# A drain behind the last matmul of every group gives TensorE's signals, in a two-layer graph network

## The chip, the cores and the metric

One core of one Trainium2 chip runs the whole program in one launch. The metric is the device time of one execution in microseconds, as the median of several runs. Engines are named as in the profile: PE (TensorE; PEld are its weight loads), DVE (VectorE), ACT (ScalarE), POOL (GpSimd), SP (SyncE).

## The reference, cut to what matters

The input is `x` (8 x 2048 x 256, float32) and an adjacency matrix `adj` (8 x 2048 x 2048, int32, here of zeros and ones, about 1.6% ones, with ones on the diagonal). Two layers follow each other:

```python
# layer 0: of each row, the first 25 neighbours; their features' maximum
vals, idx = jax.lax.top_k(where(adj != 0, -arange(N), -inf), 25)
agg = max over the 25 of x[idx]            # with 0 among them when the degree is <= 25
x = layernorm(x + relu(concat([x, agg]) @ W0 + b0))
# layer 1: four heads of 64, attention over the neighbours
h = einsum('bnd,hde->bhne', x, W1)
weight = leaky_relu(e_src[i] + e_dst[j]) where adj == 1, else -1e9
dst = softmax(weight) @ h + bias
out = per-head layernorm(relu(dst) + h) * gamma + beta
x = layernorm(x + out)
```

## The kernel before, in words

The 16384 rows are 128 tiles of 128 rows (`TILES`); four tiles (`QT`) are a quad, and 16 tiles are one batch entry. Each engine runs its own loop over quads (`run_quads`), and in it one `step(quad, u)` for each tile `u` of the quad. There is no scheduler: the order of the work on each engine is the order in which `step` writes it, and engines meet by semaphores alone. A wait compares a semaphore with a count worked out from the quad's number.

The stages stand at different tiles in one step:

- **Masks and search**, ahead. ACT turns an adjacency tile into float16 (line 518), PE transposes it in 16 pieces in two halves (line 1148, `transpose_mask`), ACT copies each half into `stage` and into the ring `maskT` (lines 543 and 547), PE packs 16 columns to a word with 16 short matmuls (line 1162, `pack_words`), and DVE finds the first 26 neighbours in a chain of 35 operations, each of which waits for the one before it (`search_words` from line 729, `top32` at lines 716 and 718, up to `idx` at line 769). Line 731 tells PE that the words are read.
- **Gather**. POOL issues 25 indirect DMAs to a tile (line 499), five to a chunk. DVE takes the maximum chunk by chunk (line 837) and frees each chunk for POOL as it goes (`s_rfree`); then it reduces (lines 846 and 847). PE transposes `x` and `agg` (line 1188, `transpose_xa`) and ACT copies the result (line 629).
- **Layer 0's product and norm**. PE multiplies (lines 1201 and 1202, `product0`), DVE adds the residual and normalizes (lines 779 to 811), PE transposes again (line 1211), ACT copies (line 641), PE multiplies by layer 1's weights (lines 1217 and 1219, `product1`), ACT takes the exponentials (lines 654 to 664, `project`).
- **Attention**, one batch entry behind. A tile's step has eight units. For a unit ACT scales two blocks (line 566), DVE masks them (line 820), and PE multiplies two heads (line 1233, `attend`). Four buffers `uv` are passed round, so ACT's unit n waits until PE is done with unit n - 4.
- **A quad's end**. At `u == 0` ACT moves the sums out of PSUM (line 587), PE transposes them (line 1172, `back`), DVE divides (lines 861 and 864, `divide`), and only then may PE start the next quad's sums (line 868 tells it); the finishing work stands between DVE's other operations.

```python
back (u == 0); product0; units 0-3; product1; units 4, 5;
transpose_mask; unit 6; pack_words; transpose_xa; unit 7
```

Of the kernel before, what the change touches and what calls it, by code (L numbers as in the profile page):

```python
# [29 lines left out]
P = 128  # L30
B, N, C = 8, 2048, 256
HEADS, HO = 4, 64
HW = HO + 1
S = 25
JT = N // P
# [10 lines left out]
WPT = P // WORD  # L46
# [106 lines left out]
def layers_program(nc, x, adj, w0, b0, w1, a_src, a_dst, bias1, gamma, beta,  # L153
# [12 lines left out]
    with ctx:  # L166
        def sb(name, shape, dt):
            return ctx.enter_context(nc.sbuf_tensor(name, shape, dt))

        def ps(name, shape, dt):  # L170
            return ctx.enter_context(nc.psum_tensor(name, shape, dt))

        def sem(name):
            return ctx.enter_context(nc.semaphore(name))

        id16 = sb("id16", [P, P], F16)
        id32 = sb("id32", [P, P], F32)
        pack = sb("pack", [P, WPT], BF16)
# [5 lines left out]
        b0_sb = sb("b0_sb", [1, C], F32)  # L185
        ones_row = sb("ones_row", [1, P], F32)
        wcat = sb("wcat", [P, 2, C + 2 * HEADS], F32)
# [8 lines left out]
        mask_sb = sb("mask_sb", [P, N], F16)  # L196
        stage = sb("stage", [P, JT, P], BF16)
# [22 lines left out]
        xh = [sb(f"xh{p}", [P, 2, C], F32) for p in range(2)]  # L220
        x1T = sb("x1T", [P, 2, P], F32)
        hs = sb("hs", [P, 2 * JT, HEADS, HW], F32)
# [6 lines left out]
        uv = [sb(f"uv{k}", [P, 2, IB], F32) for k in range(UVB)]  # L229
        sT = sb("sT", [HW, HEADS, IB], F32)  # L230
# [34 lines left out]
        acc = [ps(f"acc{i}", [P, 512], F32) for i in range(QT)]  # L265
        pT = [ps(f"pT{i}", [P, HALF * P], F16) for i in range(2)]
        pA = ps("pA", [P, 512], F32)
        pB = ps("pB", [P, 512], F32)
        p_lin, p_key = pB[:, 0:C], pB[:, 384:384 + WORDS]
        p_h = pB[:, 0:C + 2 * HEADS]  # L270
        p_ed = pB[:, C + HEADS:C + 2 * HEADS]
        p_x1T, p_es = pA[:, 0:2 * P], pA[0:HEADS, 2 * P:3 * P]
# [8 lines left out]
        s_T = sem("s_T")  # L281
        s_stage = sem("s_stage")
        s_ring = sem("s_ring")
        s_key = sem("s_key")
# [7 lines left out]
        s_xaT = sem("s_xaT")  # L292
        s_xaE = sem("s_xaE")
        s_lin = sem("s_lin")
# [7 lines left out]
        s_x1T = sem("s_x1T")  # L302
        s_x1E = sem("s_x1E")
        s_h = sem("s_h")
# [5 lines left out]
        s_pe = sem("s_pe")  # L310
        s_blk = sem("s_blk")
        s_sT = sem("s_sT")
        s_back = sem("s_back")
# [820 lines left out]
        def _(pe):  # L1134
# [3 lines left out]
            def transpose_mask(quad, u, g_of):  # L1138

                for v in quad.reach(lambda q: QT * q + u + g_of + 1):  # L1140
                    pe.wait_ge(s_mask, v)
                for hf in range(2):

                    for v in quad.reach(lambda q: 2 * (QT * q + u + g_of - 1) + hf + 1):
                        pe.wait_ge(s_ring, v)
                    for j in range(HALF):
                        jt = hf * HALF + j
                        last = nc.tensor.transpose(pT[hf][:, j * P:(j + 1) * P], mask_sb[:, jt * P:(jt + 1) * P], id16[:])
                    last.then_inc(s_T, 1)

            def pack_words(quad, u, g_of):

                for v in quad.reach(lambda q: 2 * (QT * q + u + g_of + 1)):
                    pe.wait_ge(s_stage, v)
                for v in quad.reach(lambda q: QT * q + u + g_of):
                    pe.wait_ge(s_keyread, v)

                for v in quad.reach(lambda q: QT * q + u + g_of - FRONT):
                    pe.wait_ge(s_proj, v)  # L1160
                for jt in range(JT):
                    last = nc.tensor.matmul(p_key[:, jt * WPT:(jt + 1) * WPT], stage[:, jt, :], pack[:], start=True, stop=True)
                last.then_inc(s_key, 1)

            def back(quad):

                for v in quad.reach(lambda q: q - BQ):
                    pe.wait_ge(s_sT, v)
                for i in range(QT):  # L1170
                    for h in range(HEADS):
                        last = nc.tensor.transpose(acc[i][:, h * HW:(h + 1) * HW], sT[:, h, i * P:(i + 1) * P], id32[0:HW, 0:HW])
                last.then_inc(s_back, 1)

            def transpose_xa(quad, u):

                p = u % 2

                for v in quad.reach(lambda q: QT * q + u + 1):
                    pe.wait_ge(s_agg, v)  # L1180
                for v in quad.reach(lambda q: 16 * (2 * q + u // 2 + 1)):
                    pe.wait_ge(s_x[p], v)

                for v in quad.reach(lambda q: QT * q + u):
                    pe.wait_ge(s_proj, v)
                for c in range(4):
                    src = (xt[p] if c < 2 else agg)[:, c % 2 * P:(c % 2 + 1) * P]
                    last = nc.tensor.transpose(pA[:, c * P:(c + 1) * P], src, id32[:])  # L1188
                last.then_inc(s_xaT, 1)

            def product0(quad, u):

                if quad.on(u, -AHEAD):
                    for v in quad.reach(lambda q: QT * q + u + AHEAD + 1):
                        pe.wait_ge(s_keyread, v)

                for v in quad.reach(lambda q: QT * q + u):
                    pe.wait_ge(s_xaE, v)
                for c in range(4):  # L1200
                    nc.tensor.matmul(p_lin, xaT[:, c, :], w0_sb[:, c, :], start=(c == 0), stop=False)  # L1201
                nc.tensor.matmul(p_lin, ones_row[:], b0_sb[:], start=False, stop=True).then_inc(s_lin, 1)

            def product1(quad, u):

                p = (u - 1) % 2

                for v in quad.reach(lambda q: QT * q + u):
                    pe.wait_ge(s_x1, v)
                for c in range(2):  # L1210
                    last = nc.tensor.transpose(p_x1T[:, c * P:(c + 1) * P], xh[p][:, 0, c * P:(c + 1) * P], id32[:])  # L1211
                last.then_inc(s_x1T, 1)

                for v in quad.reach(lambda q: QT * q + u):
                    pe.wait_ge(s_x1E, v)
                for c in range(2):
                    nc.tensor.matmul(p_h, x1T[:, c, :], wcat[:, c, :], start=(c == 0), stop=(c == 1))  # L1217
                for c in range(2):
                    last = nc.tensor.matmul(p_es, wcat[:, c, C:C + HEADS], x1T[:, c, :], start=(c == 0), stop=(c == 1))
                last.then_inc(s_h, 1)  # L1220

            def attend(quad, u, a, b):

                if not quad.on(u, QT * BQ):
                    return
                for n in range(a, b):
                    jt, hh, k = QT * u + n // 2, n % 2, n % UVB

                    for v in quad.reach(lambda q: UNITS * (q - BQ) + US * u + n + 1):
                        pe.wait_ge(s_u, v)  # L1230
                    for i in range(2):
                        h = 2 * hh + i
                        last = nc.tensor.matmul(acc[h][0:HW, :], hs[:, (1 - quad.par) * JT + jt, h, :], uv[k][:, i, :],  # L1233
                                                start=(jt == 0), stop=(jt == JT - 1))
                    last.then_inc(s_pe, 1)

            def step(quad, u):
                if u == 0 and quad.on(u, FIN):
# [23 lines left out]
            for g in range(FRONT):  # L1262
                transpose_mask(Quad(pe, 0, 0, 0), 0, g)
                pack_words(Quad(pe, 0, 0, 0), 0, g)
# [7 lines left out]
            with pe.If(pe.value_load(redo[0:1, 0:1], min_val=0, max_val=1) > 0):  # L1272
                with pe.Fori(0, TILES) as g:

                    pe.wait_ge(s_g1load, 16 * g + 16)
                    for c in range(2):
                        last = nc.tensor.transpose(pA[:, c * P:(c + 1) * P], xr[:, 0, c * P:(c + 1) * P], id32[:])
# [5 lines left out]
                    for c in range(2):  # L1283
                        last = nc.tensor.matmul(pA[0:TH, 2 * P:3 * P], wst[:, (2 * c + 1) * TH:(2 * c + 2) * TH], x1T[:, c, :],
                                                start=(c == 0), stop=(c == 1))
                    last.then_inc(s_g1P, 1)
                with pe.Fori(0, TILES) as g:
                    for h in range(HEADS):

                        pe.wait_ge(s_g2p, HEADS * g + h + 1)  # L1290
                        for j in range(JT):
                            last = nc.tensor.transpose(acc[j // QT][:, j % QT * P:(j % QT + 1) * P], z[:, j * P:(j + 1) * P], id32[:])
# [3 lines left out]
                        for j in range(JT):  # L1296
                            last = nc.tensor.matmul(pA[:, 0:HO], pTs[:, j * P:(j + 1) * P], hb[:, j * C + h * HO:j * C + (h + 1) * HO],
                                                    start=(j == 0), stop=(j == JT - 1))
# [52 lines left out]
```

## Time and profile before

| | |
|---|---|
| median of 3 runs | 5537.12 us (5534.57 to 5538.47) |
| the profiled execution | 5509.0 us, its span 5507.2 us |
| PE busy | 3399.5 us, 62% |
| DVE busy | 4129.9 us, 75% |
| ACT busy | 3106.5 us, 56% |
| POOL busy | 3739.9 us, 68% |
| mean granted clock of PE | 0.776 |
| HBM | 692.79 MB moved, mean 126 GB/s |

How to read it: busy time leaves out the sequencer's work, so POOL's 68% doesn't hold the part of each indirect DMA that stands in the profile as idle time before it ("issue").
### The profile page before, as it was taken

The numbers are of one execution on the slowest core, as the hardware profiler recorded it, in microseconds if no ns is written. First come the engines' busy times: TensorE is split into PE (matmuls) and PEld (weight loads), VectorE is DVE, ScalarE is ACT, GpSimd is POOL, SyncE is SP. The second block draws the span as 40 slices with busy tenths as digits, with TensorE's granted clock in tenths as the row PEclk, the third lists the DMA queues.
The fourth block names the chain that finished last, engine by engine and source line by source line (L and its number), as shares of the span: only waits on it lengthen the run. The fifth ranks groups of instructions, "written<-read, shape, count | busy, mean of one in ns | idle before, by whom it ended". The sixth has DMA issues, their size and how long they took to land.

```text
span 5507.2 us, 58308 instructions
## 1 busy us (share of the span) xinstructions
PE 3399.5 (62%) x11778; PEld 1421.4 (26%) x11778; DVE 4129.9 (75%) x11484; ACT 3106.5 (56%) x5570; POOL 3739.9 (68%) x3204
## 2 busy tenths in 40 slices
PE   1233266676666765666666666675576665756786
PEld 1112122222222322222222222222222222322222
DVE  4455468787787876978877877786788787967777
ACT  3233356565565655656655665664566565755565
POOL 4666677777787776877776777776677776877400
PEclk9555577787877877878877877777787787877898
DMA  3333344444444444434444444443444444444210
GB/s 122 116 121 114 121 141 132 140 123 137 133 146 127 143 133 124 146 123 148 135 134 127 144 131 129 135 142 112 132 135 150 123 135 127 146 128 129 81 38 27
DMA packets 282031, 692.79 MB, mean 126 GB/s; under 512 B 62849, under 2 KB 130178, under 8 KB 265346
## 3 DMA queue, kind: packets, MB, share of 16 engines
q0 software_dynamic: 153600, 419.64, 26.2%
q1 hardware_dynamic: 128130, 270.41, 15.1%
q14 instruction: 267, 2.19, 0.1%
q8 instruction: 34, 0.56, 0.0%
HBM read 639.21 MB, written 50.59 MB: 125 GB/s over the span
## 4 chain that ended last, share of the span: by engine, by line
DVE 27%; issue 19%; POOL 16%; PE 15%; another core or an unknown queue 12%; ACT 9%; DMA 1%; ACTq 0%; DVEq 0%; POOLq 0%; SPq 0%
POOL rows L499 16%; PE acc L1233 8%; DVE uv L820 8%; DVE rmax L837 4%; ACT uv L566 4%; DVE top L716 2%; PE pB L1201 2%; DVE agg L846 2%; DVE key_b L718 2%; PE pB L1217 1%; ACT stage L526 1%; ACT maskT L547 1%; DMA rows<-in_x_dram,idx 1%; DVE key_a L718 1%
## 5 line engine op out<-in xcount | busy, mean ns | idle before, releaser
L499 POOL DMA_INDIRECT rows<-in_x_dram,idx x3200 | 3739.7, 1169 | 1437.6 <-issue 1039.0
L1233 PE MATMUL acc<-uv,hs 128*65 128x512 f32 x4096 | 2253.1, 700 | 562.3 <-DVE uv L820 326.7
L820 DVE SCALAR_TENSOR_TENSOR uv<-uv,maskT 128x1024 f32<-128x1024 f32 x1024 | 1241.2, 1222 | 390.3 <-ACT uv L566 245.2
L566 ACT ACTIVATE uv<-rb,qj 128x512 f32 (+1 forms) x2048 | 1327.4, 711 | 240.0 <-PE acc L1233 143.6
L1233 PEld LDWEIGHTS acc<-uv,hs 128*65 128x65 f32 x4096 | 596.1, 158 | 1836.4 <-issue 1410.3
L837 DVE TENSOR_TENSOR rmax<-rmax,rows 128x1280 f32<-128x1280 f32 x384 | 569.2, 1482 | 118.2 <-DMA rows<-in_x_dram,idx 106.0
L1201 PE MATMUL pB<-w_sb,xaT 128*128 128x256 f32 x1024 | 369.0, 523 | 294.0 <-DVE pad L731 153.7
L629 ACT ACTIVATE xaT<-pA 128x512 f32<-128x512 f32 x128 | 76.4, 597 | 728.8 <-remote 392.6
L543 ACT ACTIVATE stage<-pT 128x1024 bf16<-128x1024 f16 x256 | 258.9, 1011 | 255.8 <-remote 142.8
L1201 PEld LDWEIGHTS pB<-w_sb,xaT 128*128 128x128 f32 x1024 | 264.9, 270 | 454.1 <-DVE pad L731 211.2
L596 ACT ACTIVATE sd<-mv,eps 128x1 f32<-128x1 f32 x128 | 37.7, 295 | 515.7 <-DVE tick L792 433.6
L846 DVE TENSOR_REDUCE agg<-rmax 128x256 f32<-128x1280 f32 x128 | 299.2, 2337 | 7.4 <-remote 1.6
L1188 PE MATMUL pA<-id,xt 128*128 128x128 f32 x256 | 75.9, 392 | 360.8 <-DVE agg L847 211.1
L641 ACT ACTIVATE x1T<-pA 128x256 f32<-128x256 f32 x128 | 49.1, 383 | 420.6 <-PE pA L1211 242.2
L1211 PE MATMUL pA<-id,xh 128*128 128x128 f32 x256 | 64.4, 340 | 349.0 <-DVE xh L811 336.6
L1217 PE MATMUL pB<-wcat,x1T 128*128 128x264 f32 x512 | 196.7, 520 | 118.8 <-ACT x1T L641 70.3
L547 ACT ACTIVATE maskT<-pT 128x1024 f16 (+1 forms) x256 | 258.8, 1011 | 0.0
L779 DVE SCALAR_TENSOR_TENSOR r<-pB,xt 128x256 f32<-128x256 f32 x128 | 53.3, 416 | 272.8 <-remote 189.0
L526 ACT ACTIVATE stage<-adj_sb,minus 128x2048 bf16<-128x2048 int32 x128 | 254.3, 1986 | 1.2 <-remote 1.2
L518 ACT ACTIVATE mask_sb<-adj_sb 128x2048 f16<-128x2048 int32 x128 | 243.0, 1898 | 3.7 <-DMA adj_sb<-in_adj_dram 3.2
L716 DVE MAX8 top<-key_a 128x8 f32<-128x104 f32 (+1 forms) x768 | 209.9, 273 | 40.9 <-remote 8.6
L716 DVE MAX8 top<-key_b 128x8 f32<-128x104 f32 (+1 forms) x768 | 207.4, 270 | 41.6 <-remote 24.7
(113 smaller groups left out, 3904.5 us busy)
## 6 DMA issues: line engine op xcount, KB each, us to landing
adj_sb<-in_adj_dram SPq DMA_DIRECT2D x128, 1024.0 KB
rows<-in_x_dram,idx POOLq DMA_INDIRECT x3200
xh_dram<-xh SPq DMA_DIRECT2D x128, 256.0 KB
rb<-r_dram SPq DMA_DIRECT2D x32, 1024.0 KB
xr<-xh_dram SPq DMA_DIRECT2D x64, 512.0 KB
xt<-in_x_dram SPq DMA_DIRECT2D x128, 128.0 KB
out_dram<-xr SPq DMA_DIRECT2D x32, 512.0 KB
r_dram<-er SPq DMA_DIRECT2D x128, 2.0 KB
```

The costliest lines, as they stand in the source:

```text
L499: nc.gpsimd.indirect_dma_start(rows[:, c, r * C:(r + 1) * C], None, x_rows, bass.IndirectOffsetOnAxis(ap=idx[u][:, k:k + 1], axis=0)).then ...
L526: nc.scalar.activation(stage[:].rearrange("p j i -> p (j i)"), adj_sb[:], ACT.Square, scale=2.0, bias=minus1[:], accum_out=adj_sq[:, bass. ...
L543: nc.scalar.activation(stage[:, hf * HALF:(hf + 1) * HALF, :], src, ACT.Square).then_inc(s_stage, 1)
L547: nc.scalar.activation(maskT[:, bass.ds(qg % RING * JT + hf * HALF, HALF), ug * P:(ug + 1) * P], src, ACT.Square).then_inc(s_ring, 1)
L566: last = nc.scalar.activation(uv[k][:, i, :], rb[:, bass.ds(qa % 2, 1), h, :].rearrange("p a i -> p (a i)"), ACT.Copy, scale=q_j(h))
L716: ch.then(nc.vector.max(top[:, k:k + 8], a))
L820: nc.vector.scalar_tensor_tensor(uv[k][:], uv[k][:], 1.0, m, ALU.max, ALU.mult).then_inc(s_u, 1)
L837: nc.vector.tensor_tensor(rmax[:], before, rows[:, c, :], ALU.max).then_inc(s_rfree, 2 if c == 1 else 1)
L846: ch.then(nc.vector.tensor_reduce(agg[:], rmax[:].rearrange("p (r f) -> p f r", f=C), axis=AX.X, op=ALU.max))
L1201: nc.tensor.matmul(p_lin, xaT[:, c, :], w0_sb[:, c, :], start=(c == 0), stop=False)
L1217: nc.tensor.matmul(p_h, x1T[:, c, :], wcat[:, c, :], start=(c == 0), stop=(c == 1))
L1233: last = nc.tensor.matmul(acc[h][0:HW, :], hs[:, (1 - quad.par) * JT + jt, h, :], uv[k][:, i, :], start=(jt == 0), stop=(jt == JT - 1))
```

## The change

Each group's increment is taken off its last matmul and put on a drain that follows it on PE's queue. The drain is an instruction of its own in PE's queue: it is to pass when the engine has finished what was given to it before, and then it gives the increment. The order of matmuls, all waits and all counts stay as they are; no other engine's program changes. One place stands for all, with the two that read otherwise:

```diff
                     for j in range(HALF):
                         jt = hf * HALF + j
-                        last = nc.tensor.transpose(pT[hf][:, j * P:(j + 1) * P], mask_sb[:, jt * P:(jt + 1) * P], id16[:])
-                    last.then_inc(s_T, 1)
+                        nc.tensor.transpose(pT[hf][:, j * P:(j + 1) * P], mask_sb[:, jt * P:(jt + 1) * P], id16[:])
+                    pe.drain().then_inc(s_T, 1)
...
-                nc.tensor.matmul(p_lin, ones_row[:], b0_sb[:], start=False, stop=True).then_inc(s_lin, 1)
+                nc.tensor.matmul(p_lin, ones_row[:], b0_sb[:], start=False, stop=True)
+                pe.drain().then_inc(s_lin, 1)
...
                     for i in range(2):
                         h = 2 * hh + i
-                        last = nc.tensor.matmul(acc[h][0:HW, :], hs[:, (1 - quad.par) * JT + jt, h, :], uv[k][:, i, :],
+                        nc.tensor.matmul(acc[h][0:HW, :], hs[:, (1 - quad.par) * JT + jt, h, :], uv[k][:, i, :],
                                                 start=(jt == 0), stop=(jt == JT - 1))
-                    last.then_inc(s_pe, 1)
+                    pe.drain().then_inc(s_pe, 1)
```

`s_key`, `s_back`, `s_xaT`, `s_x1T` and `s_h` are changed in the same way. Over the program that is 8 x 128 + 7 x 128 + 32 = 1952 drains.

## Rows read from the trace of the kernel before

**Rows 1.** The page: busy time of each engine, granted clock, chain that ended last.

```profile
span 5507.2 us, 58308 instructions
...
PE 3399.5 (62%) x11778; PEld 1421.4 (26%) x11778; DVE 4129.9 (75%) x11484; ACT 3106.5 (56%) x5570; POOL 3739.9 (68%) x3204
...
PEclk9555577787877877878877877777787787877898
...
DVE 27%; issue 19%; POOL 16%; PE 15%; another core or an unknown queue 12%; ACT 9%; DMA 1%; ACTq 0%; DVEq 0%; POOLq 0%; SPq 0%
```

**Rows 2.** The page's groups: busy, mean ns | idle before, releaser.

```profile
L499 POOL DMA_INDIRECT rows<-in_x_dram,idx x3200 | 3739.7, 1169 | 1437.6 <-issue 1039.0
...
L1233 PE MATMUL acc<-uv,hs 128*65 128x512 f32 x4096 | 2253.1, 700 | 562.3 <-DVE uv L820 326.7
```

**Rows 3.** The waits, whole span: who waited for whom, us, times, longest.

```profile
POOL rows L499 <- DVE rmax L837: 355.3, 40, 16.8
...
ACT xaT L629 <- remote: 392.6, 32, 29.0
...
DVE r L779 <- remote: 189.0, 31, 21.5
...
DVE key_b L729 <- remote: 165.9, 19, 26.2
...
ACT stage L543 <- remote: 142.8, 35, 17.1
...
DVE rden L861 <- remote: 89.6, 11, 13.4
...
POOL rows L499 <- DVE idx L769: 43.4, 1, 43.4
```

**Rows 4.** Timeline, 1963 to 1989 us: start, us, engine, line [idle before <-releaser].

```profile
1965.72 2.00 PE L1172 MATMUL acc<-id,sT 65*128 65x65 f32 x16 [9.36 <-issue]
...
1967.51 3.73 PE L1201 MATMUL pB<-w_sb,xaT 128*128 128x256 f32 x8
...
1971.17 0.88 PE L1202 MATMUL pB<-b_sb,ones_row 1*128 1x256 f32 x2
...
1981.66 0.39 DVE L861 RECIPROCAL rden<-acc 128x4 f32<-128x4 f32 x4 [13.45 <-remote]
...
1988.39 0.94 POOL L499 DMA_INDIRECT rows<-in_x_dram,idx  x1 [10.49 <-DVE rmax L837]
```

**Rows 5.** Timeline, 263 to 273 us.

```profile
262.36 0.59 PE L1162 MATMUL pB<-pack,stage 128*128 128x8 bf16 x16 [29.07 <-ACT stage L543]
...
263.27 0.63 PE L1188 MATMUL pA<-id,agg 128*128 128x128 f32 x2
...
267.60 0.95 POOL L499 DMA_INDIRECT rows<-in_x_dram,idx  x1 [0.30 <-issue]
...
272.58 0.29 DVE L729 SCALAR_TENSOR_TENSOR key_b<-pB,wordkey 128x128 f32<-128x128 f32 x1 [15.58 <-remote]
...
272.64 0.60 ACT L629 ACTIVATE xaT<-pA 128x512 f32<-128x512 f32 x1 [9.42 <-remote]
```

**Rows 6.** Timeline of a step without such a wait, 3000 to 3028 us.

```profile
3000.09 0.38 PE L1211 MATMUL pA<-id,xh 128*128 128x128 f32 x2
...
3000.51 0.38 ACT L641 ACTIVATE x1T<-pA 128x256 f32<-128x256 f32 x1 [2.23 <-PE pA L1211]
...
3000.94 1.16 PE L1217 MATMUL pB<-wcat,x1T 128*128 128x264 f32 x4 [0.47 <-ACT x1T L641]
...
3006.30 1.93 PE L1233 MATMUL acc<-uv,hs 128*65 128x512 f32 x4 [1.81 <-DVE uv L820]
...
3013.00 3.43 PE L1233 MATMUL acc<-uv,hs 128*65 128x512 f32 x4 [3.87 <-DVE uv L820]
...
3025.75 7.08 PE L1233 MATMUL acc<-uv,hs 128*65 128x512 f32 x16
```

**Rows 7.** Windows: two steps without such a wait, and the one of rows 4.

```profile
core 0: us, PE busy (x) PEld busy (x) DVE busy (x) ACT busy (x) POOL busy (x), PEclk, DMA share, GB/s
...
3166.00:3201.20 35.20, 25.46 (x88) 10.33 (x88) 32.44 (x79) 23.43 (x43) 28.12 (x23) 0.84 0.41 127
...
3201.20:3236.10 34.90, 25.29 (x88) 10.20 (x88) 30.60 (x83) 25.01 (x44) 27.91 (x23) 0.79 0.41 128
...
1964.00:2008.00 44.00, 25.89 (x96) 12.02 (x96) 23.71 (x69) 20.83 (x39) 26.51 (x25) 0.72 0.33 103
```

**Rows 8.** Window of the tail after the last gather, line 1233 alone.

```profile
5190.00:5507.00 317.00, 236.52 (x516) 71.35 (x516) 0.90 0.12 38
```

**Rows 9.** Timeline of PE within the tail.

```profile
5301.14 13.95 PE L1233 MATMUL acc<-uv,hs 128*65 128x512 f32 x32 [0.73 <-DVE uv L820]
5317.03 17.71 PE L1233 MATMUL acc<-uv,hs 128*65 128x512 f32 x40 [1.93 <-DVE uv L820]
```

More of the change, by code:

```diff
@@ L1161, in pack_words @@
                 for jt in range(JT):
-                    last = nc.tensor.matmul(p_key[:, jt * WPT:(jt + 1) * WPT], stage[:, jt, :], pack[:], start=True, stop=True)
-                last.then_inc(s_key, 1)
+                    nc.tensor.matmul(p_key[:, jt * WPT:(jt + 1) * WPT], stage[:, jt, :], pack[:], start=True, stop=True)
+                pe.drain().then_inc(s_key, 1)
             def back(quad):
@@ L1171, in back @@
                     for h in range(HEADS):
-                        last = nc.tensor.transpose(acc[i][:, h * HW:(h + 1) * HW], sT[:, h, i * P:(i + 1) * P], id32[0:HW, 0:HW])
-                last.then_inc(s_back, 1)
+                        nc.tensor.transpose(acc[i][:, h * HW:(h + 1) * HW], sT[:, h, i * P:(i + 1) * P], id32[0:HW, 0:HW])
+                pe.drain().then_inc(s_back, 1)
             def transpose_xa(quad, u):
@@ L1187, in transpose_xa @@
                     src = (xt[p] if c < 2 else agg)[:, c % 2 * P:(c % 2 + 1) * P]
-                    last = nc.tensor.transpose(pA[:, c * P:(c + 1) * P], src, id32[:])
-                last.then_inc(s_xaT, 1)
+                    nc.tensor.transpose(pA[:, c * P:(c + 1) * P], src, id32[:])
+                pe.drain().then_inc(s_xaT, 1)
             def product0(quad, u):
@@ L1210, in product1 @@
                 for c in range(2):
-                    last = nc.tensor.transpose(p_x1T[:, c * P:(c + 1) * P], xh[p][:, 0, c * P:(c + 1) * P], id32[:])
-                last.then_inc(s_x1T, 1)
+                    nc.tensor.transpose(p_x1T[:, c * P:(c + 1) * P], xh[p][:, 0, c * P:(c + 1) * P], id32[:])
+                pe.drain().then_inc(s_x1T, 1)
                 for v in quad.reach(lambda q: QT * q + u):
@@ L1218, in product1 @@
                 for c in range(2):
-                    last = nc.tensor.matmul(p_es, wcat[:, c, C:C + HEADS], x1T[:, c, :], start=(c == 0), stop=(c == 1))
-                last.then_inc(s_h, 1)
+                    nc.tensor.matmul(p_es, wcat[:, c, C:C + HEADS], x1T[:, c, :], start=(c == 0), stop=(c == 1))
+                pe.drain().then_inc(s_h, 1)
             def attend(quad, u, a, b):
```

## The prediction

> **What bounds the kernel now.** I read the page first, for the shares; then the groups; then the waits, longest first; and last the timeline, at the places that the waits name.
>
> No engine is full [rows 1]: DVE has 75%, POOL 68%, PE 62%. The chain that ended last puts 12% of the span on "another core or an unknown queue", in a program with one core. So something on this core releases work in a way that the profile can't tie to an instruction.
>
> POOL is fuller than it looks [rows 2]: 3200 gathers at 1169 ns, and 1039.0 us of "issue" between them, are 4778.7 us. With its waits for DVE, 355.3 us, and the one at the start, 43.4 us [rows 3], that makes 5177.4 us; what is left of the span is the tail without gathers. POOL's own work is therefore the floor under the time, and the 355.3 us are the most that the part up to the last gather can give back.
>
> What holds DVE, when POOL waits for it? The waits with the releaser "remote" are all of instructions that wait for a signal of PE [rows 3]: line 629 (`s_xaT`) 392.6 us in 32 waits, line 779 (`s_lin`) 189.0, line 729 (`s_key`) 165.9, line 543 (`s_T`) 142.8, line 861 (`s_back`) 89.6. Three of the five stand on DVE: 444.5 us in 61 waits.
>
> The timeline shows what such a wait is. PE's transposes of a quad's end are over at 1965.72 + 2.00 = 1967.72 us, and PE goes on to product 0, whose last matmul ends at 1972.05 [rows 4]. Line 861 on DVE, which needs the first of these, starts at 1981.66, 13.9 us late and after 13.45 us of idleness; PE itself did not stall, since it ran 4.6 us of later matmuls. POOL then idled 10.49 us for want of a free chunk. Near the start it is plainer still [rows 5]: the words end at 262.95, the transposes of `agg` at 263.90, POOL's last gather at 268.55, and after that nothing runs until lines 729 and 629 start together, 0.06 us apart, at 272.58 and 272.64. Two signals that were due 0.95 us apart come at once, 9 us late. **Increments attached to matmuls are held back now and then, and then let go together.**
>
> It is not so with other signals, and mostly not with PE's. In a quiet step ACT starts 0.04 us after PE's transposes (3000.09 + 0.38 to 3000.51), and PE 0.05 us after ACT (3000.89 to 3000.94) [rows 6]. Steps without a held signal take 35.2 and 34.9 us and PE is busy for 25 of them; the stretch that holds the late one has 44.0 us for the same 25.9 us of PE [rows 7].
>
> **The change part by part.** It removes 1952 attached increments and adds 1952 drains, each with one increment. Nothing is moved on any queue; what stands behind a drain is all of PE's later work, its weight loads too, and whoever waits for that.
>
> *What the drain costs.* The trace has no drain in this place. The lower bound is the overlap of one matmul's end with the next one's start: four units back to back take 7.08 us and one alone takes 1.93 us [rows 6], so each of the three others adds (7.08 - 1.93) / 3 = 1.72 us, and 0.21 us of a unit's end is overlapped. The upper bound is a whole trip through another engine: between the transposes of line 1211 and the matmuls of line 1217, PE idles 0.47 us, and in it ACT gets a signal, copies for 0.38 us and sends one back [rows 6]; with the overlapped end (0.21) that makes 0.68 us. Register work for the next unit, which now runs ahead, will run behind the drain, so I take 0.4 us, between the two.
>
> *Where it lies beside other work.* A full step has 15 drains, 6 us of PE. A quiet step leaves PE 35 - 25.3 = 9.7 us of idle time [rows 7], and POOL needs 25 x (1169 + 325) ns = 37.4 us for a step's gathers (325 ns is 1039.0 us over 3200) [rows 2]. So PE, with 25.3 + 6 = 31.3 us, and DVE, with its 35 us, both stay under POOL. In the body I cost the drains at nothing; POOL's gathers hide them. If that cover is gone (a step in which DVE and not POOL is last), a drain costs its delay at the five or so hand-overs to DVE and ACT that stand in a step's chain, up to 2 us a step.
>
> *Where it doesn't.* In the tail there are no gathers, and PE is the bound: 236.52 us of 317 in line 1233 [rows 8], 40 records in 17.71 us, thus (17.71 - 0.21) / 10 = 1.75 us a unit [rows 9]. 516 records are 129 units; with 0.4 us each +52 us (bounds: 0.21 gives +27, 0.68 gives +88).
>
> *What the held signals give back.* If an increment that the sequencer gives is not held, the waits called "remote" go. DVE's 444.5 us can't all come back, because POOL is next: the body gains POOL's waits for DVE, 355.3 us at most. I leave 55 us of them, since DVE's quad starts are longer than other steps and POOL must wait there when it is no longer behind. Gain: -300 us. POOL's mean of 1169 ns stays, because the slower gathers among them are slowed by DVE's operations, and these are as many as before.
>
> *Sum.* 5509 - 300 + 52 = 5261 us for an execution like the profiled one. That one lies 28 us under the median of the runs shown (5537), so I give 5289, rounded to **5290 us**.
>
> *A rule of the Trainium skill against the change.* What the rows show is that an attached increment can arrive 9 to 14 us after the work [rows 4, 5]. The Trainium skill's "PSUM — Partial Sum Buffer", section "Engine vs sequencer instructions", says to attach the increment to the matmul itself, and names a drain, which waits until the engine is idle, only for a standalone barrier. By that rule nothing is to be gained here and the sum would hold only the drains' costs, which is the first rival. The rows speak against it in this kernel.
>
> **The rivals.**
>
> *The drain's increment is held like the others* (slower). What is held may be the way from PE to the semaphores, whoever sends. For it: I can't see in the trace why they are held. Against it: only an attached increment has been seen late here. Then the waits stay, and the drains cost 52 us in the tail and some 0.5 us in each of 128 steps, the part that falls where no cover is: 64 us. 5537 + 52 + 64 = 5653 us. It decides as soon as less than 116 of the 300 us are given back.
>
> *It is the completion that is held, not the increment* (slower, more). If PE has not been told that its writes have landed, the drain waits through the hold, and what PE now does in the meantime comes after it: 4.6 us behind `s_back` in rows 4. With 3 us for each of DVE's 61 waits, 183 us more: 5653 + 183, about 5840 us. Against it: two groups' signals come together after an idle machine [rows 5], and matmuls go on through the hold [rows 4].
>
> *The clock falls* (slower). PE's granted clock is 0.79 to 0.84 in quiet steps and 0.72 in the slow stretch [rows 7]; it stands at 1.2 GHz after PE has waited, where a unit takes 3.43 us in place of 1.93 [rows 6]. Drains put holes into the runs of units. At a mean of 0.6 a step's matmuls take 25.3 x 0.79 / 0.6 = 33.3 us, with the drains 39.3, more than POOL's 37.4; in the tail, where the clock is 0.90 [rows 8], 129 units cost 1.75 x (0.90 / 0.6 - 1) + 0.4 = 1.28 us more each, +165. That gives 5537 - 300 + 128 x 1.9 + 165 = about 5645 us. The point from which it decides is a clock of 0.79 x 25.3 / 31.4 = 0.64. Against it: a unit with its drain still keeps PE busy 1.72 us out of 2.1, and the long idle stretches go. The Trainium skill's "TensorE: Matmul & The Clock Gate", Part 1, says that the clock follows how busy the engine has been, which would let it fall to the lower level if the holes count; no row here shows a run with such holes.
>
> *Part of the holds go and the drains take it back* (same). DVE's search chain has a few late signals of its own and they may keep the quad starts slow. Then -110 and +116: 5540 us.
>
> **How the numbers follow.** My forecast has 62%: the held signals are the clearest thing in the trace, they name one engine's attached increments, and the idle machine of rows 5 leaves little else. The drain's increment held too: 14%. Completion held: 10%. Clock: 6%. Taken back in part: 8%, of which one point comes out faster and seven within the bound. A measurement of this kernel tells about 0.2% from no change, 11 us. So faster 63%, same 7%, slower 30%.
>
> The range: the forecast's own best end is 5537 - 355 + 27 = 5209 us, and 28 us less for a run like the profiled one, thus 5180. Its own worst end is 5537 - 200 + 88 = 5425. To hold 8 in 10 it must reach past the case of 5540 and the first rival at 5653, so to 5680. The likeliest case alone would be 5180 to 5425.
>
> **What would show it.** In the profile of the changed kernel: the rows with "remote" for lines 629, 779, 729, 543 and 861 fall from about 980 us together to under 100; POOL's wait for line 837 falls from 355 us to about 55; the last gather ends near 4880 us and not near 5177; DVE's share rises toward 79%. The runs of 16 records in line 1233 take 3 x 0.4 = 1.2 us longer than 7.08, and 40 records in the tail 9 x 0.4 = 3.6 us longer than 17.71. I am wrong if the "remote" waits stay (first rival), if PE's own matmuls stop during them (second), if the mean clock is under 0.65 (third), or if a unit in the tail takes over 2.5 us, when the drain's price was mis-sized.

## The result, and the profile after

The changed kernel takes **5933.89 us** (median of 4 runs, 5861.19 to 6006.61), the kernel before, run beside it, 5537.8 us (4 runs): a ratio of 1.0621 (95% interval 1.0527 to 1.0715). Medians here are of all runs of a kernel; ratios and intervals are of its fast runs alone, those within 1.5% of its fastest one. By the medians it is 396 us slower, and outside my range. The profiled execution took 5954.52 us, 445.5 us more than the profiled one before.

```profile
span 5952.7 us, 60260 instructions
PE 3620.4 (61%) x11778; PEld 1360.6 (23%) x11778; DVE 4142.8 (70%) x11484; ACT 3130.3 (53%) x5570; POOL 3698.8 (62%) x3204
PEclk9555678777787777787777877787877777778898
issue 55%; DVE 17%; PEld 13%; PEldq 8%; ACT 4%; POOL 1%; another core or an unknown queue 1%; DMA 0%; ACTq 0%; DVEq 0%; SPq 0%; POOLq 0%; PE 0%
L499 POOL DMA_INDIRECT rows<-in_x_dram,idx x3200 | 3698.6, 1156 | 1899.9 <-issue 1018.0
```

The chain has turned from work (POOL 16%, PE and DVE lines behind it) into 55% "issue", time in which the profile sees nobody being waited for, and 8% PEldq, the drains themselves.

The waits of the changed kernel, answering to [rows 3] (us, times, longest):

```profile
POOL rows L499 <- DVE rmax L837: 836.9, 99, 21.6
ACT xaT L629 <- PEq L1189: 715.7, 98, 25.6
PE pA L1188 <- issue: 582.5, 107, 17.5
DVE r L779 <- PEq L1203: 306.0, 105, 16.0
DVE key_b L729 <- PEq L1163: 288.9, 65, 16.4
ACT stage L543 <- PEq L1149: 214.5, 86, 19.7
DVE rden L861 <- PEq L1173: 61.0, 14, 8.0
```

All waits called "remote" at these five lines are gone, and each stands there again with a drain as its releaser: 1586 us together, where before "remote" was 980 us and PE's own lines 337 us. POOL's wait for DVE rose by 836.9 - 355.3 = 482 us; its gathers became 41 us shorter in sum (1156 in place of 1169 ns) and its "issue" 21 us. That makes 420 us, and the last gather's end moved by 421: from 5177.79 to 5598.90 us. The tail behind it grew by 24 us, from 329.4 to 353.8; the two make up the 445 us between the profiled executions.

Not all "remote" is gone. DVE waits in this way for its own results too, in a chain with no instruction of PE: 57.5 us in 25 waits before, 88.7 us in 41 after. The largest of these, before and after:

```profile
DVE top L716 <- remote: 33.3, 14, 3.7
```

```profile
DVE top L716 <- remote: 46.7, 22, 4.6
```

One step of the changed kernel on the timeline, PE from 2870 to 2884 us and then DVE, and one key drain asked for by its line:

```profile
2872.85 0.57 PE L1162 MATMUL pB<-pack,stage 128*128 128x8 bf16 x16 [0.33 <-issue]
2879.74 0.66 PE L1188 MATMUL pA<-id,xt 128*128 128x128 f32 x2 [6.33 <-issue]
2880.20 0.63 PE L1188 MATMUL pA<-id,agg 128*128 128x128 f32 x2
```

```profile
2872.78 2.35 DVE L820 SCALAR_TENSOR_TENSOR uv<-uv,maskT 128x1024 f32<-128x1024 f32 x2
2879.36 0.29 DVE L729 SCALAR_TENSOR_TENSOR key_b<-pB,wordkey 128x128 f32<-128x128 f32 x1 [4.22 <-issue]
```

```profile
L1163 PEldq DRAIN  x1: 6403/6403/6403, 2872.9 to 2872.9; - x1
```

The sixteen short matmuls of the key end at 2873.42. The drain behind them ends at 2872.92 + 6.40 = 2879.32, DVE starts 0.04 us after it, and PE has stood for 6.33 us, with `agg` ready since 2872.86. In the kernel before, DVE waits for such a signal too, but PE goes on: in [rows 4] it ran 4.6 us of later matmuls in such a hold. This is my second rival, by the sign that I gave for it (PE's own matmuls stop).

Over the program, taking for each drain its end less the end of the last matmul ahead of it, 397 of the 1952 drains last over 0.5 us longer than the matmuls, together 1430 us: 117 of the 128 at the key (572 us, the longest 17.2), 109 of the 256 at `s_T` (417 us), 67 of the 1024 in attend (153 us). Of the others, all but 55 end 0.02 us after the last matmul.

### The profile page after: what moved, and what is told of

It reads as the page before. It is cut to its first block, busy times and chain, and to the rows that moved or that the text cites. A ratio compares the mean times of both kernels' runs of the same rounds, so it can differ in the third digit from the quotient of the medians.

```text
span 5952.7 us, 60260 instructions
## 1 busy us (share of the span) xinstructions
PE 3620.4 (61%) x11778; PEld 1360.6 (23%) x11778; DVE 4142.8 (70%) x11484; ACT 3130.3 (53%) x5570; POOL 3698.8 (62%) x3204
## 3 DMA queue, kind: packets, MB, share of 16 engines
q0 software_dynamic: 153600, 419.64, 23.9%
## 4 chain that ended last, share of the span: by engine, by line
issue 55%; DVE 17%; PEld 13%; PEldq 8%; ACT 4%; POOL 1%; another core or an unknown queue 1%; DMA 0%; ACTq 0%; DVEq 0%; SPq 0%; POOLq 0%; PE 0%
PEld acc L1234 5%; DVE uv L820 4%; DVE rmax L837 3%; PEld pB L1201 3%; PEldq L1236 3%; ACT uv L566 2%; PEldq L1203 2%; DVE top L716 2%; POOL rows L499 1%; DVE key_b L718 1%; PEldq L1149 1%; PEld pT L1148 1%; PEld pA L1188 1%; PEld pB L1162 1%
## 5 line engine op out<-in xcount | busy, mean ns | idle before, releaser
L499 POOL DMA_INDIRECT rows<-in_x_dram,idx x3200 | 3698.6, 1156 | 1899.9 <-issue 1018.0
L1234 PE MATMUL acc<-uv,hs 128*65 128x512 f32 x4096 | 2384.6, 712 | 719.0 <-issue 580.5
L1234 PEld LDWEIGHTS acc<-uv,hs 128*65 128x65 f32 x4096 | 550.4, 156 | 2175.4 <-issue 1961.4
L629 ACT ACTIVATE xaT<-pA 128x512 f32<-128x512 f32 x128 | 76.4, 597 | 887.0 <-PEq L1189 715.7
L1201 PE MATMUL pB<-w_sb,xaT 128*128 128x256 f32 x1024 | 395.1, 553 | 231.4 <-issue 219.9
L1148 PE MATMUL pT<-id,mask_sb 128*128 128x128 f16 x2048 | 170.7, 231 | 216.1 <-issue 182.8
L729 DVE SCALAR_TENSOR_TENSOR key_b<-pB,wordkey 128x128 f32<-128x128 f32 x128 | 36.8, 288 | 313.4 <-PEq L1163 288.9
```

The costliest lines, as they stand in the source:

```text
L499: nc.gpsimd.indirect_dma_start(rows[:, c, r * C:(r + 1) * C], None, x_rows, bass.IndirectOffsetOnAxis(ap=idx[u][:, k:k + 1], axis=0)).then ...
```

## The experiments

They were run on several chips, and this turned out to matter more than the change. On two chips the kernel **before** takes 5096 and 5098 us and not 5537; the edits traced there show no hold and not one wait called "remote". On four others it took 5501 to 5567 us, as in the first measurement. I call them chips without and with holds. Each chip was seen in one job only, so what is called a chip's here may be the job's.

### Chips without holds

**The change itself.** Unedited.

> The change itself once more, beside the kernel before on the same chip. In the first four runs the kernel before took 5097 us on the chip they ran on, not 5537, and no completion was held there: gathers end at about 4775 us. Theory H (the loss of the change is PE standing in drains while completions are held): on a chip without holds the change costs only the drains' own price, 5120 to 5150 us against 5097, most of it in the tail; on a chip with holds it is again 5860 to 6000 against 5537. Theory D (the drains' own price): 300 us or more over the kernel before on either.

Measured: 5143.17 us (5135.52 to 5148.19) against 5095.94, ratio 1.0088 (1.0071 to 1.0105). Its key drains, by min/median/max in ns, and two of its waits:

```profile
L1163 PEldq DRAIN  x128: 345/508/550, 30.2 to 4686.5; - x128
```

```profile
POOL rows L499 <- issue: 974.7, 3199, 0.3
ACT xaT L629 <- PEq L1189: 851.9, 128, 26.1
```

No drain is longer than its matmuls (median 508 ns here, 4514 in the first measurement), and POOL never waits for DVE: all 3199 gaps between gathers are issue, the longest 0.3 us. The last gather ends at 4793.0 us. With nothing held, the drains cost 47 us. ACT's 851.9 us of waiting at line 629 are more than the 715.7 of the first measurement and delay nobody that counts: a long sum of waits for a drain is no sign of a hold by itself.

**Increment attached, bare drain behind it**, for all 1952 groups:

```diff
-                    pe.drain().then_inc(s_T, 1)
+                    last.then_inc(s_T, 1)
+                    pe.drain()
```

> The increments stay attached to the last matmuls as before, and a bare drain without increment stands behind each of the 1952 groups. Theory H (matmuls are told complete late, and PE stands in the drain meanwhile): as slow as the change, 5860 to 6000 us, with the held time in the drains of the lines of pack_words and transpose_mask; a signal attached to the matmul and the end of the drain behind it come together. Theory S (the change is slow because a drain's increment comes later than an attached one): back near 5540 to 5650 us, since signals are attached again.

Measured: 5136.44 us against 5097.52, ratio 1.0079 (1.0062 to 1.0096). The same as the change: the cost is PE's standing, not where the increment hangs.

**Drains in attend only**, the other lines as before.

> Only the 1024 groups of attend give their signal by a drain; the other 928 keep the attached increment. Theory H: the change's drains of attend were held in 67 cases for 153 us of the 1420 us that all were held, so most of the loss is gone: 5600 to 5720 us, of which about 55 us in the tail (0.42 us for each of 129 units). Theory D (each drain costs its own price, about 0.4 us, wherever it stands): half of the drains are here, so about half of the loss, 5700 to 5760 us.

Measured: 5126.51 us, ratio 1.0055 (1.0038 to 1.0073). Both bands were for a chip with holds.

**Drains outside attend only**, attend as before.

> Only the 928 groups outside attend give their signal by a drain; attend keeps attached increments. Theory H: nearly the whole loss of the body stays and the tail is as before: 5780 to 5900 us. Theory D: about half of the loss, 5700 to 5760 us.

Measured: 5096.69 us, ratio 0.9999 (0.9989 to 1.001), last gather at 4770.4 us. So 928 drains are worth nothing where POOL is the floor, as the prediction had it, and 1024 in attend cost 29 us. Most of that is the tail: from the last gather to the end it is 350.5 us with attend's drains and 325.0 without.

**Pack's sixteen matmuls run twice** (`for jt in tuple(range(JT)) * 2`), to see whether more matmuls behind a held one let it go.

> The change with the 16 short matmuls of pack_words issued twice over (same result). If the drain behind them is long (median 4.5 us) because these matmuls run slowly, it gets about 4 us longer, near 8.5 us, and the kernel is some 300 to 500 us slower. If it is long because the report of completion is held after the work (theory H), it grows by the work alone, 0.4 to 1.7 us, and the kernel stays within 100 us of the change.

Measured: 5145.12 us. Nothing is held on this chip, so it says nothing about that.

**The gathers left out**, of the change and of the kernel before; the gathered rows are set to zero once at the start, and POOL gives the gathers' increments without them:

```diff
-                        nc.gpsimd.indirect_dma_start(rows[:, c, r * C:(r + 1) * C], None, x_rows, ...).then_inc(s_rows[c], 16)
+                    pool.sem_inc(s_rows[c], 16 * CR)
```

> The change without the gathers: POOL gives their increments at once, and rows stays zero (the neighbours' maximum is left out). Only of use on a chip with holds. If the gathers cause the holds, no drain ends more than 0.3 us after its last matmul, as after the last gather in the change, where none did; if they come from PE's own short matmuls or from DVE's search, the drains of pack_words stay at a median near 4.5 us. Without holds: about 4500 to 4800 us, bound by DVE's 35 us a step.

> The kernel before without the gathers, as a partner of the change without them: the difference of the two is the drains' price where POOL doesn't cover it. With 15 drains of 0.42 us a step, some of them on the path: 20 to 150 us less than the change without gathers.

Measured: 4658.44 us for the change, 4516.41 for the kernel before. Without POOL's cover the drains cost 142 us, three times as much (one run of each; 145 us in the pair further down).

**Gathers replaced by plain DMAs from SP**, of as many bytes, but always of the first 128 rows of x, and without the wait for the indices.

> The change with the gathers replaced by plain DMAs of the same size from SP's queue (always the first 128 rows; the choice of neighbours is left out), nothing on POOL. On a chip with holds: if POOL's issuing is the cause the holds go; if it is the traffic into SBUF they stay. Without holds the time tells only SP's pace, 3200 issues, 5000 to 6500 us.

Measured: 4667.28 us. That is under the 5000 to 6500 that I gave: I had taken SP's issues for slower than they are. As nothing is held here anyway, it only shows that as many bytes without POOL's gathers cost 9 us.

### Chips with holds

**Two drains in place of one**, a bare one first.

```diff
+                pe.drain()
                 pe.drain().then_inc(s_key, 1)
```

> Each of the 1952 groups gets a bare drain ahead of the drain that gives the signal. Two kinds of chip have to be told apart. On one like those of the runs before this (the kernel before near 5097 us): if what a drain costs is the lost overlap between one unit's last matmul and the next one's first (0.42 us in the trace of the change, of which 0.02 us is the drain and 0.21 us the restart), a second drain that finds PE empty adds only some tens of ns and the kernel ends within 10 us of the change's 5143 us; if each drain has a price of its own, the kernel pays again in attend what the change paid, and ends near 5190 us. On a chip like that of the first measurement (before at 5537 us): if a drain lasts as long as the completion ahead of it is held, the first drain of the two takes the whole hold, the second about 20 ns, and the kernel ends near the change's 5934 us; if drains are what is held, each on its own account, the second is held as often as the first and the kernel ends above 6200 us.

Measured: 5953.17 us (5908.7 to 6014.78) against 5567.4, ratio 1.0777 (1.0587 to 1.0967). Both drains of the key, asked for by line:

```profile
L1164 PEldq DRAIN  x128: 472/4396/27613, 30.0 to 5550.3; - x128
```

```profile
L1165 PEldq DRAIN  x128: 13/13/13, 30.6 to 5559.3; - x128
```

The first takes all of the hold, its longest 27.6 us with the matmuls in it; the second takes 13 ns every time. So a drain is not held on an account of its own: what the first waits for is there for the second as well. The second is not quite free: it moves the end of the pair from 0.02 to 0.10 us behind the last matmul, and a unit in the tail from 2.14 to 2.21 us.

**Increment attached, bare drain behind it**, again.

> The increments hang on the last matmuls as in the kernel before, and a bare drain that gives nobody anything stands behind each. On a chip with held completions (the kernel before at 5480 to 5580 us): if the loss of the change comes from PE standing in the drain until the held completion is in, this kernel loses the same and ends at 5880 to 6020 us, with bare drains of several us at the key's and the pack's lines; if the loss comes from where the increment hangs (a sequencer's increment passed on late), it stays within 60 us of the kernel before. On a chip without holds (before near 5097 us): 5136 us as in the first run of it.

Measured: 5973.7 us against 5557.02, ratio 1.0693 (1.05 to 1.0886): the change's whole loss, with every increment where it was before. The timeline of one step, PE and DVE, and the drain in it:

```profile
3005.43 0.54 PE L1163 MATMUL pB<-pack,stage 128*128 128x8 bf16 x16 [2.42 <-issue]
3019.89 0.66 PE L1191 MATMUL pA<-id,xt 128*128 128x128 f32 x2 [13.91 <-issue]
```

```profile
3019.50 0.29 DVE L729 SCALAR_TENSOR_TENSOR key_b<-pB,wordkey 128x128 f32<-128x128 f32 x1 [13.82 <-remote]
```

```profile
L1165 PEldq DRAIN  x1: 14007/14007/14007, 3005.5 to 3005.5; - x1
```

This kernel has both signs in one: the **attached** increment arrives 13.5 us late and is called "remote", and the drain ends at 3005.50 + 14.01 = 3019.51, 0.01 us after DVE has got that increment. Late increment and long drain are the same event, and this drain gives no increment, so it isn't the way of an increment that is slow. What is held is the matmuls' completion. Whether they finish late or are only told late can't be read here, as the end of a matmul is modelled in the trace.

**Drains outside attend only**, again.

> 928 drains outside attend, attend as in the kernel before. On a chip with held completions: if the time goes by the us that PE stands in held drains, the trace of the change puts some 1260 of its 1420 us of held drains at the lines outside attend, so this kernel should lose most of what the change loses, 250 to 400 us over the kernel before; if the loss is that of the drains' number and of the tail (half of the drains, all of the tail's price is attend's), it loses under 60 us. On a chip without holds: within 10 us of the kernel before.

Measured: 5629.03 us against 5557.02, ratio 1.0191 (1.0048 to 1.0334). I expected 250 to 400 us more, or under 60, and got 72 (27 to 186 by the interval). Its drains lasted 1243 us longer than their matmuls, in 311 cases, nearly as in the change. So the held time of the drains is not what the change pays. That most of it passes while nobody is in want of PE's next work would explain it; no run shows this by itself.

**Drains in attend only**, again.

> Only the 1024 groups of attend carry their drain. On a chip with held completions (the kernel before at 5480 to 5580 us): there the 928 other drains alone cost 72 us although they lasted 1200 us longer than PE's work. If it is attend's drains that carry the rest, by 0.42 us each on a chain that POOL no longer covers, this kernel ends at 5780 to 5950 us (the change's loss less 72 us, up to 1024 x 0.42 = 430 us); if the two halves only cost together, it ends below 5700 us. On a chip without holds (before near 5097 us): 5126 us as in the first run of it.

Measured: 5758.3 us (5657.89 to 5877.43) against 5527.04 (5505.68 to 5600.06), 231 us more. That lies between my two bands (5780 to 5950, and under 5700), and the four runs are 220 us apart, the lower two 5679 us in the mean, so it doesn't decide between them. The drains of attend, by line:

```profile
L1235 PEldq DRAIN  x1024: 1748/1948/21390, 703.2 to 5625.4; - x171
```

Now these drains meet the holds: 123 of them last over 0.5 us too long, 574 us in all, where in the change 67 did. A drain waits for whatever completion is still out when it is reached. By the medians the two halves add up to 303 us of the 396, with 80 us and more of uncertainty in each. That the rest needs both halves together is not shown.

**The gathers left out**, again, before and change:

> The gathers are left out, so the rows that are gathered are zero. On a chip with held completions: if the gathers on POOL and their descriptors are what holds PE's completions, none is held here and the time is near the 4516 us of the chip without holds; if the holds belong to PE's own completions whatever POOL does, waits for PE's signals (called remote) of 100 us and more stay for s_T, key and pack, and the time is 4750 us or more. On a chip without holds: 4516 us within 0.3%.

> The change with the gathers left out (the gathered rows are zero). On a chip with held completions: if the gathers hold them, every drain ends within 0.1 us of the last matmul and the time is near the 4658 us of the chip without holds; if not, drains of 1 to 17 us stand at key, s_T and pack as in the trace of the change, and the time is 5000 us or more. On a chip without holds: 4658 us within 0.3%.

Measured: 4516.9 and 4662.03 us, within 4 us of the chip without holds. The key's drains in the change, by line:

```profile
L1160 PEldq DRAIN  x128: 364/490/550, 30.0 to 4224.2; - x128
```

None is held, and in the kernel before no wait with the releaser "remote" is left. On the same chip, in the same job, before with gathers took 5557 us. **Without the gathers nothing is held.**

**Bytes or instruction?** Plain DMAs of as many bytes from SP, and the same from POOL:

```diff
-                        nc.gpsimd.indirect_dma_start(rows[:, c, r * C:(r + 1) * C], None, x_rows, ...).then_inc(s_rows[c], 16)
+                        nc.gpsimd.dma_start(rows[:, c, r * C:(r + 1) * C], x_rows[0:P, :]).then_inc(s_rows[c], 16)
```

> The change with each gather replaced by a plain DMA of as many rows, issued from SP (so other rows than the reference's are read). On a chip with held completions: if it is the bytes and DMA packets of the rows that hold PE's completions, drains of 1 to 17 us stay and the time is 5000 us or more; if it is the gather instruction of POOL (its descriptors, written by POOL itself), no drain is held and the time is near the 4667 us of the chip without holds. On a chip without holds: 4667 us within 0.3%.

> As the run before, but the plain DMAs are issued from POOL. On a chip with held completions: if any DMA that POOL issues, descriptors and all, holds PE's completions, drains of 1 to 17 us are seen and the time is 4900 us or more; if only the indirect form does, no drain is held and the time is within 150 us of the one issued from SP. On a chip without holds: no drain held.

Measured: 4670.53 and 4684.0 us, with the kernel before at 5527 us on the same chip. From the page of the one that POOL issues, and its key's drains:

```profile
q0 software_dynamic: 153600, 419.64, 28.0%
```

```profile
L1160 PEldq DRAIN  x128: 336/490/548, 30.1 to 4246.3; - x128
```

It is the same queue with the same 153600 packets and 419.64 MB as in the change, and nothing is held. So it is neither the bytes nor that queue. A plain DMA takes POOL less time, though (busy 1692 us in place of 3699), and no run has separated the indirect form from the time that it takes.

**The gathers kept, all indices 0.**

```diff
-                            bass.IndirectOffsetOnAxis(ap=idx[u][:, k:k + 1], axis=0)).then_inc(s_rows[c], 16)
+                            bass.IndirectOffsetOnAxis(ap=same[:, k:k + 1], axis=0)).then_inc(s_rows[c], 16)
```

> The change with POOL's indirect gathers kept, but all their indices 0, so every gather fetches row 0 of x for all partitions (not the neighbours' rows). On a chip with held completions: if the indirect instruction as such holds PE's completions, whatever addresses it fetches, drains of 1 to 17 us stay, the waits for drains come back and the time is above 5300 us; if the scattered addresses do, none is held and the time is that of the chips without holds, near 5143 us, where POOL's own floor sets it. On a chip without holds: 5143 us within 1%, no drain held, and nothing is told apart.

Measured: 6360.36 us, the kernel before beside it 5500.59. Its key's drains by line, and from its page the gathers' queue:

```profile
L1165 PEldq DRAIN  x128: 545/4561/21030, 30.9 to 5870.9; - x128
```

```profile
q0 software_dynamic: 153600, 419.64, 74.0%
```

The holds are as before: median 4561 ns at the key, 358 drains over 0.5 us too long, 1291 us in all. Scattering isn't needed; POOL's indirect instruction as such is enough. The 426 us above the change go with slower packets: these, all for one row, took 74% of the DMA engines' time in place of 23.9%, and DVE waited 399 us for gathered rows in place of 27.

No version beat the kernel before.

## Why the prediction was wrong, point by point

- **What bounds the kernel, and POOL's floor**: right. On chips without holds POOL has this floor and nothing above it. By the trace of the run with drains outside attend only (the kernel before has none there), its gathers and "issue" are 4727 us and the last gather ends at 4770.4; from my 4778.7 and the 43.4 at the start it would be 4822. So [rows 3] were right about the loss from late signals too, and too low: 5537 against 5097 us is 440 us. The 355.3 us of POOL's waits are most of it, and I should not have left 55 of them; the longest "issue" wait of POOL was 16.5 us before and is 0.3 us there, and the sum went from 1039.0 to 975, 64 us more, against 12 us by which the gathers got longer.
- **The failed step** is in "What the held signals give back": "If an increment that the sequencer gives is not held, the waits called 'remote' go." The condition is true, the increment of a drain comes at the drain's end (0.04 us to DVE's start in the step above). But the drain itself waits for the completion that is held (its end 13.54 us after the matmuls when the attached increment came 13.5 us late). The term of -300 us was not small or lost, it had the wrong sign: POOL's waits for DVE rose by 482 us.
- **Where I misread the rows**: I took "increments attached to matmuls are held back" from [rows 4, 5]. These rows show only that a waiter got its signal late. That two signals come 0.06 us apart I held against a held completion; it fits one as well, if a hold of the first completion keeps back the second, and no row excluded that. I also wrote that the waits called "remote" are all for a signal of PE. DVE's 57.5 us of them for its own results are not, and with them "one engine's attached increments" was too narrow; they too are there only with gathers, on chips with holds.
- **The second rival** (completion held, 10%) named the mechanism and 5840 us. The size was off: I charged 3 us for each of DVE's 61 waits, 183 us more than the first rival's 5653. Measured are 396 us over the median, against 303 forecast. The 3 us were an assumption, and near 400 us is partly luck. What it leaves out is that PE's stop also delays what ACT wants next: ACT waited 430 us for attend's drains at line 566, where before it waited 208 us there (144 for PE's line, 64 "remote"). The two halves show that the loss isn't the sum of held time: 1243 us of it outside attend cost 72 us, 574 us in attend together with the drains' own price 231.
- **What a drain costs**: right. In the tail, ten units in a row, answering to [rows 9]:

```profile
5700.96 1.93 PE L1234 MATMUL acc<-uv,hs 128*65 128x512 f32 x4 [0.22 <-issue]
5703.10 1.93 PE L1234 MATMUL acc<-uv,hs 128*65 128x512 f32 x4 [0.21 <-issue]
...
5720.38 1.93 PE L1234 MATMUL acc<-uv,hs 128*65 128x512 f32 x4 [0.21 <-issue]
```

  They last 5720.38 + 1.93 - 5700.96 = 21.35 us against 17.71, so 3.64 us more; I had written 3.6. A unit costs 2.14 us in place of 1.72 (one of the nine here 2.30): the overlap of 0.21 us is lost, and PE idles 0.21 us more until the next matmul. A unit is four records there, two to a product; what the two stand for, no trace here shows.
- **The tail, +52 us**: mis-sized. It grew by 24 us (353.8 against 329.4 us between last gather and end). I charged all 129 units; PE's weight loads of line 1233 waited 54.0 us for line 820 in the tail before and 38.1 us after, so it seems that part of the price fell into idle time; the rest of the difference is not accounted for.
- **Hidden in the body under POOL**: right where POOL is the floor (928 drains: ratio 0.9999), with a remainder that I had at nothing: on the chip without holds, POOL's gathers are 3774.9 us in the change and 3751.9 in the kernel whose attend has no drains, and by these 23 us the last gather ends later (4793.0 against 4770.4). On chips with holds POOL is not the floor in many steps and the cover is gone, the very condition that the text named.
- **The clock**: not it. The mean is 0.764 in the profiled change and was 0.776 before, far from the 0.64 at which it would decide, and in the tail 0.91 with a drain behind every unit, against 0.90 in [rows 8].
- **The spread.** I took 0.2% as what a measurement can tell, from three runs 4 us apart. Seven later runs of the kernel before on one chip lie between 5489 and 5583 us, 1.7% apart.
- **The sign I had set** for my forecast was bad. "Remote" fell from 980 us to nothing while the kernel got slower: the change gave the profile a name for the releaser, and not the waiter its data.
- The rule of the Trainium skill that I had weighed ("PSUM — Partial Sum Buffer", section "Engine vs sequencer instructions": the increment on the matmul, a drain for a standalone barrier) is given there for the sake of right results and not of speed. The runs agree with it on speed too: no version with drains was faster. The attached increment with a bare drain cost as much as the change, so it is the barrier that has its price.

## What to carry to other kernels

A late signal can mean a late notice or a late completion. Before an instruction that waits for completion is put in the signal's place, find one that already stands behind such work and see how long it takes. In the step traced here the drain gave the signal no earlier than the attached increment, and it stopped all that was queued behind it. Where a kernel has software gathers and its short matmuls are waited for, look at whether the same kernel without the gathers loses its waits of unknown origin; and run it on more than one chip before a wait is taken for a property of the kernel. An instruction's price in isolation (0.42 us here) becomes a loss only where nothing covers it: the same 1952 drains cost 47 us under POOL's gathers and 142 us without them.

## What the runs showed of the hardware that I had not expected

- While POOL runs indirect gathers, PE's completions can be held, in these runs up to 27.4 us behind the matmuls (increment attached, bare drain behind it); plain DMAs of as many packets on the same queue hold none, and gathers of a single row do as well as scattered ones. Before the first gather and after the last no drain of these lines was held, in the trace of the change and in those of all five edits with gathers on chips with holds.
- It isn't PE's alone: DVE got its own results late, up to 3.7 us in the kernel before at line 716, in traces with gathers on chips with holds and in no other.
- It happened on some chips, or in some jobs, only. The same kernel took about 5097 us on two chips and 5501 to 5567 on four, with gathers of nearly the same length (1172 ns with drains outside attend only, 1169 in the kernel before). What differs between them, and by what path a gather holds a completion, stays open. A hold doesn't end with a gather in particular: 256 of the 397 in the change end in the midst of one, and POOL is busy for 62% of the span.
- A drain that finds nothing outstanding takes 13 ns by its own record, and moved the end behind it by 0.07 to 0.08 us.
- Whether a later matmul helps a held completion out wasn't settled, since that run fell on a chip without holds.
